# Three stages of a layered transformer kernel: residual sums written straight into the resident stream

## The chip, the cores and the metric

The kernel runs on one core of a Trainium2 chip. The metric is the time of one execution on the device, in microseconds (us); lower is better. All engines of the core run their own instruction streams and meet at semaphores: TensorE (PE) multiplies and transposes, VectorE (DVE), ScalarE (ACT) and GpSimd (POOL) compute on tiles, SyncE (SP) issues the transfers.

## What is computed

A batch of 32 sequences of 64 tokens with 128 features goes through four layers, each of a mixing step and a feed-forward step. Every step adds its result to the running x and takes the layer norm of x as its input. Cut to the steps around the change:

```python
def _layernorm(x, axis=-1, eps=1e-05):
    m = jnp.mean(x, axis=axis, keepdims=True)
    v = jnp.var(x, axis=axis, keepdims=True)
    return (x - m) / jnp.sqrt(v + eps)

x = x + _L0_xattn_ref(_layernorm(x), ctx_1024, ctx_1024, ...)   # gated recurrence: stage lstm
x = x + _L0_ffn_ref(_layernorm(x), ...)                          # mixture, 8 experts: stage moe0
x = x + _L1_xattn_ref(_layernorm(x), ctx_1024, _lenS2, ...)      # attention: stage att1
x = x + _L1_ffn_ref(_layernorm(x), ...)                          # mixture with shared expert: stage moe1
...                                                              # two further layers
```

Everything is fp32.

## The kernel before, in words

All 2048 tokens stay in SBUF for the whole run. `x_all` (128 x 16 x 128, fp32) is the resident stream x, `xT_all` the transposed layer norm of x. The tokens go in eight pairs of tiles (`PAIRS`), 256 tokens each; `pair(x_all, p)` is the 128 x 256 slice of pair p. The stages run one after the other, each over all pairs, in software loops (`Fori`) in which the loop's register gives the pair, with a first and a last pass outside the loop. The order of the work of each engine is written out by hand, and every dependence is a semaphore; inside DVE a `drain` stands between an instruction and one that reads its result.

Each stage ends a pair in the same way. DVE forms the new x of the pair, takes its statistics (`norm_stats`: two `bn_stats` L301, two `bn_aggr` L304, then the variance plus epsilon into `var`, L306, which releases POOL). POOL computes the inverse root (`take_root`, L332). DVE then applies it (`norm_apply`, two instructions at L313) into `xn`; TensorE transposes `xn` (L343) and ACT stores it in `xT_all` (L354). In the code this is a first part (sum and statistics) and an `ending`, with other work of DVE between them, and in the loops both belong to the pair before the current one.

Where the new x is formed:

- stage lstm: `scaled` adds the recurrence's result and x into the buffer `xr` (L626), takes the statistics of `xr`, and then copies `xr` into `x_all` (L629). After it come `scans` (from L565) or `ending`.
- stage moe0: `add_up` sums the experts into `xr` (two reductions, L810), adds x (L812), adds the bias product from the PSUM bank `ybank` (L815), copies `xr` into `x_all` (L817), then takes the statistics. `weigh` (from L772) follows, then `ending`, then `combine` (L802), which empties the banks that TensorE fills at L712.
- stage att1: `end_residual()` without a bias gives the two parts: the sum of `ybank` and x into `xr` (L1643), the copy `keep_stream` (L1637), the statistics. `divide` (L1388) scales queries and keys for TensorE's transposes (L1241) between the two parts.
- stage moe1, which the change doesn't touch: `sum_up` adds `ybank` into `x_all` in place (L1034), and statistics and `norm_apply` read `x_all` itself.

`end_residual("l3_bout")` of a later stage, ffn2 and tern keep `xr`, since they write x plus a bias into the stream (L1635) while the norm reads x without it.

Of the kernel before, what the change touches and what calls it, by code (L numbers as in the profile page):

```python
# [19 lines left out]
ALU = mybir.AluOpType  # L20
# [13 lines left out]
BUMP = 64  # L34
# [58 lines left out]
def build_program(nc, wpack, x_in, ctx_in, ctxT_in, rows_in, moeb_in, lens_in, mask_in, tern_in, scale_in, out,  # L93
                  layers=8):
    es = ExitStack()
    with es:
        def sb(name, shape, dt=F32):
            return es.enter_context(nc.sbuf_tensor(name, shape, dt))

        def sem(name):  # L100
            return es.enter_context(nc.semaphore(name))
# [12 lines left out]
        x_all = sb("x_all", [P, TILES, D])  # L114
# [3 lines left out]
        neg_len = sb("neg_len", [P, T])  # L118
# [7 lines left out]
        xn = sb("xn", [P, 2, D])  # L126
        xr = sb("xr", [P, 2, D])
# [27 lines left out]
        def bank(i):  # L155
            return big[:, i, :]

        ybank = bank(6)[:, 0:PT].rearrange("p (u d) -> p u d", u=2)
# [5 lines left out]
        def row(name, n=2):  # L164
            i = ROWS.index(name)
            return rows[:, i:i + 1, :].to_broadcast([P, n, D])

        def pair(ap3, p):

            return ap3[:, bass.ds(2 * p, 2), :]  # L170
# [15 lines left out]
        y_filled = sem("y_filled")  # L186
        xn_ready = sem("xn_ready")
        xt_filled = sem("xt_filled")
# [18 lines left out]
        def pipelined(these, mixing, inputs, late, tail=[]):  # L207


            s = stage([])  # L210
            s.pro = stage(inputs + late, 1)
            s.body = stage(these + inputs + mixing + late + tail, PAIRS - 1)
            s.epi = stage(these + mixing + tail, 1)
            return s
# [10 lines left out]
        def moe_units(nu, nd, lag):  # L225
# [4 lines left out]
            for d in downs:  # L230
# [4 lines left out]
                if d == nd - 1:  # L235
# [8 lines left out]
        att1 = pipelined(scores4, mixing8, [(f"tok{u}{c}", "a") for u in range(2) for c in range(4)],  # L244
                         values4 + [(f"turn{u}{c}", "av"[c % 2]) for u in range(2) for c in range(4)])
# [51 lines left out]
        def norm_stats(v, src, held=main):  # L297

            st, mv, var, _ = held
            for u in range(2):  # L300
                v.bn_stats(st[:, u, :], src[:, u, :])  # L301
            v.drain()
            for u in range(2):
                v.bn_aggr(mv[:, u, :], st[:, u, :])  # L304
            v.drain()
            v.tensor_scalar(var, mv[:, :, 1], 1e-5, None, ALU.add).then_inc(var_ready, 1)  # L306

        def norm_apply(v, src, dst, value, held=main):

            _, mv, _, rstd = held  # L310
            v.wait_ge(rstd_ready, value)
            for u in range(2):
                ins = v.tensor_scalar(dst[:, u, :], src[:, u, :], mv[:, u, 0:1], rstd[:, u:u + 1],  # L313
                                      ALU.subtract, ALU.mult)
            return ins
# [10 lines left out]
        def root(s, p, k):  # L326
            return p * roots[s][1] + (roots[s][0] + k)
# [28 lines left out]
        def g_of(s, p):  # L356

            return p + PAIRS * stages_run.index(s)
# [57 lines left out]
        lstm_n2 = work[:, 4864:5120].rearrange("p (g e) -> p g e", g=8)  # L416
# [137 lines left out]
        def lstm_vector(v):  # L554
            s = lstm
# [64 lines left out]
            def scaled(p):  # L620
                v.wait_ge(*h_lstm["hroot"].at(p, 1))
                v.tensor_tensor(lstm_n, lstm_n, lstm_hq[:, :, None].to_broadcast([P, 8, 32]), ALU.mult)
                v.drain()
                v.tensor_tensor(lstm_n2, lstm_n, lstm_ow.rearrange("p u (h e) -> p (u h) e", h=4), ALU.mult)
                v.drain()
                v.tensor_tensor(xr[:], lstm_n2.rearrange("p (u h) e -> p u (h e)", u=2), pair(x_all, p), ALU.add)  # L626
                v.drain()
                norm_stats(v, xr)
                v.tensor_copy(pair(x_all, p), xr[:])  # L629

            def ending(p):
                v.wait_ge(xt_filled, g_of(s, p) + BUMP)
                norm_apply(v, xr, xn, root(s, p, 1)).then_inc(xn_ready, 1)

            def part(ring, i, p, this, nxt, last=True):
                v.drain()
                if this:
                    exponent(ring, i)
                if nxt:
                    magnitude(ring, i, p + 1)  # L640
                if this:
                    decayed(ring, i, p)
                if this and last:
                    scaled(p - 1)
                if nxt:
                    scans(p + 1)
                if this:
                    if last:
                        ending(p - 1)
                    divided(ring, i, p)  # L650
            steps_lstm(v, part)
            scaled(PAIRS - 1)
            ending(PAIRS - 1)


# [13 lines left out]
        def moe(tag, s, pre, experts, chunks, func, layer):  # L669
# [70 lines left out]
            def vector(v):  # L740
# [66 lines left out]
                def add_up(p):  # L807

                    for u in range(2):
                        v.reduce_sum(xr[:, u, :], pr[:, u, :, :].rearrange("p e d -> p d e"), AX)  # L810
                    v.drain()
                    v.tensor_tensor(xr[:], xr[:], pair(x_all, p), ALU.add)  # L812
                    v.drain()
                    v.wait_ge(y_filled, p + yb(s))
                    v.tensor_tensor(xr[:], ybank, xr[:], ALU.add)  # L815
                    v.drain()
                    v.tensor_copy(pair(x_all, p), xr[:])  # L817
                    norm_stats(v, xr)

                def ending(p):  # L820
                    v.wait_ge(xt_filled, g_of(s, p) + BUMP)
                    ins = norm_apply(v, xr, xn, root(s, p, 1))
                    if layer == 1:
                        v.drain()
                        ins = v.tensor_tensor(pair(tok_all, p), xn[:], row("sa_bo"), ALU.add)
                    ins.then_inc(xn_ready, 1)

                def step(p, last=True):
                    v.drain()
                    sort(p)  # L830
                    if last:
                        add_up(p - 1)
                    weigh(p)
                    if last:
                        ending(p - 1)
                    combine(p)
# [4 lines left out]
                with v.Fori(1, PAIRS) as p:  # L841
                    step(p)
                add_up(PAIRS - 1)
                ending(PAIRS - 1)

            def pool(g, p):
# [235 lines left out]
        def yb(s):  # L1082

            return ystages.index(s) * PAIRS + 1
# [546 lines left out]


        def keep_stream(v, p, bias):
            if bias:
                v.tensor_tensor(pair(x_all, p), xr[:], row(bias), ALU.add)  # L1635
            else:
                v.tensor_copy(pair(x_all, p), xr[:])  # L1637

        def end_residual(bias=None):

            def first_part(v, s, p):
                v.wait_ge(y_filled, p + yb(s))
                v.tensor_tensor(xr[:], ybank, pair(x_all, p), ALU.add)  # L1643
                v.drain()
                keep_stream(v, p, bias)
                norm_stats(v, xr)

            def second_part(v, s, p):
                v.wait_ge(xt_filled, g_of(s, p) + BUMP)
                norm_apply(v, xr, xn, root(s, p, 1)).then_inc(xn_ready, 1)  # L1650
            return first_part, second_part
# [82 lines left out]
        def ffn_vector(v):  # L1734
# [7 lines left out]
            def step(p, last=True):  # L1742
                v.drain()
                v.wait_ge(y_filled, p + yb(s))
                v.tensor_tensor(xd, ybank, pair(tok_all, p), ALU.add).then_inc(y_read.sem, 1)
                v.drain()
                norm_stats(v, xd, inner)
                if last:
                    outer(p - 1)
                norm_apply(v, xd, xd, root(s, p, 1), inner)  # L1750
                v.drain()
                v.tensor_tensor(xd, xd, row("ln3_g"), ALU.mult)
                v.drain()
                v.tensor_tensor(xd, xd, row("ln3_b"), ALU.add)
                v.drain()
                v.tensor_tensor(xr[:], xd, pair(x_all, p), ALU.add)
                v.drain()
                norm_stats(v, xr)
                keep_stream(v, p, "tern_b")
# [95 lines left out]
        h3["values"] = Handoff("l3_values", 1)  # L1855
        h3["spread"] = Handoff("l3_spread", 2)
        end3 = end_residual("l3_bout")


# [367 lines left out]
        prog = {}  # L2227
# [8 lines left out]
        if moe0 in run:  # L2236
            prog[moe0] = moe("m0", moe0, "m0", 8, 2, ACT.Gelu, 0)
        if att1 in run:
            prog[att1] = attention("a1", att1, "a1_wq", "a1_wk", "a1_wv", "a1_wo", True, 2, neg_len, end_residual())
        if moe1 in run:  # L2240
            prog[moe1] = moe_shared(moe1)
        if satt in run:
# [326 lines left out]
```

## Time and profile before

| | us |
|---|---|
| median of 3 runs | 1338.88 |
| lowest, highest | 1337.35, 1341.19 |
| the profiled execution | 1337.23 |
| its span, first to last instruction | 1335.5 |

| engine | busy us | share of the span | instructions |
|---|---|---|---|
| PE | 1049.8 | 79% | 11888 |
| DVE | 927.0 | 69% | 2053 |
| ACT | 600.0 | 45% | 1169 |
| POOL | 215.0 | 16% | 226 |

The profile is of one execution. By the order of time, stage lstm runs from about 43 to 164 us, moe0 to about 305, att1 to about 555, moe1 to about 668. Busy shares are averages over stages with different limits; what a change in a stage is worth is read from the chain of work that ended last and from the order of time in that stage.

### The profile page before, as it was taken

The numbers are of one execution on the slowest core, as the hardware profiler recorded it, in microseconds if no ns is written. First come the engines' busy times: TensorE is split into PE (matmuls) and PEld (weight loads), VectorE is DVE, ScalarE is ACT, GpSimd is POOL, SyncE is SP. The second block draws the span as 40 slices with busy tenths as digits, with TensorE's granted clock in tenths as the row PEclk, the third lists the DMA queues.
The fourth block names the chain that finished last, engine by engine and source line by source line (L and its number), as shares of the span: only waits on it lengthen the run. The fifth ranks groups of instructions, "written<-read, shape, count | busy, mean of one in ns | idle before, by whom it ended". The sixth has DMA issues, their size and how long they took to land.

```text
span 1335.5 us, 32718 instructions
## 1 busy us (share of the span) xinstructions
PE 1049.8 (79%) x11888; PEld 823.5 (62%) x11888; DVE 927.0 (69%) x2053; ACT 600.0 (45%) x1169; POOL 215.0 (16%) x226
## 2 busy tenths in 40 slices
PE   1666499997888888589989999879999672588756
PEld 1433388884655656478867787658787551366646
DVE  3788757778899989445557676686867378666645
ACT  1333244446666666233346665346665230144333
POOL 2222322220012110223100000000000121243100
PEclk9756599998999999689999999899999796599868
DMA  9200000000000000000000000000000000000001
GB/s 365 105 0 0 1 0 0 0 0 1 2 0 0 0 0 1 1 1 0 1 2 1 0 0 1 2 2 0 0 0 1 1 0 0 0 1 0 0 1 31
DMA packets 4891, 17.48 MB, mean 13 GB/s; under 512 B 601, under 2 KB 2786, under 8 KB 4194
## 3 DMA queue, kind: packets, MB, share of 16 engines
q1 hardware_dynamic: 4834, 16.70, 3.3%
q8 instruction: 38, 0.62, 0.2%
q14 instruction: 19, 0.16, 0.0%
HBM read 15.65 MB, written 1.05 MB: 13 GB/s over the span
## 4 chain that ended last, share of the span: by engine, by line
PE 33%; issue 23%; DVE 23%; DVEq 13%; ACT 2%; POOL 2%; POOLq 1%; PEldq 1%; PEld 0%; ACTq 0%
PE banks L1480 5%; PE banks L1518 3%; PE banks L1490 3%; DVEq L1135 3%; PE banks L934 3%; PE banks L712 3%; PE banks L1467 2%; PE banks L1147 2%; DVE small L1378 2%; DVE small L1109 1%; DVEq L1108 1%; PE banks L1506 1%; DVE xn L313 1%; DVE weights L1388 1%; PE banks L343 1%
## 5 line engine op out<-in xcount | busy, mean ns | idle before, releaser
L332 POOL TENSOR_TENSOR rstd<-var,nhalf 128x2 f32<-128x2 f32 x72 | 57.4, 798 | 521.0 <-DVE var L306 514.1
L343 PE MATMUL banks<-ident,xn 128*128 128x128 f32 x160 | 38.6, 330 | 86.8 <-DVE xn L313 50.3
L1568 ACT ACTIVATE work<-banks 128x512 f32<-128x512 f32 x128 | 74.7, 600 | 70.4 <-PE banks L1480 70.4
L354 ACT ACTIVATE xT_all<-banks 128x256 f32 (+1 forms) x80 | 31.3, 391 | 153.9 <-PE banks L343 152.9
L1128 ACT ACTIVATE work<-work 128x1024 f32<-128x1024 f32 x64 | 67.7, 1057 | 59.8 <-DVEq L1124 32.8
L1480 PE MATMUL banks<-xT_all,weights 128*128 (+1 forms) x384 | 86.3, 381 | 1.4 <-ACT work L1561 0.9
L1603 DVE TENSOR_TENSOR work<-banks,neg_mask 128x512 f32<-128x512 f32 x64 | 40.7, 685 | 64.1 <-PE banks L1467 63.6
L343 PEld LDWEIGHTS banks<-ident,xn 128*128 128x128 f32 x160 | 20.4, 160 | 102.1 <-DVE xn L313 46.5
L1147 PE MATMUL banks<-ident,work 128*128 128x128 f32 x512 | 69.6, 286 | 16.3 <-DVE work L1138 11.1
L735 ACT ACTIVATE work<-banks,weights 128x256 f32<-128x256 f32 x128 | 53.8, 471 | 62.3 <-PE banks L702 61.4
L1480 PEld LDWEIGHTS banks<-xT_all,weights 128*128 128x128 f32 x384 | 71.9, 191 | 13.3 <-issue 1.8
L1147 PEld LDWEIGHTS banks<-ident,work 128*128 128x128 f32 x512 | 61.1, 147 | 23.0 <-DVE work L1138 13.8
L1518 PEld LDWEIGHTS banks<-weights,work 128*128 128x128 f32 x512 | 59.3, 194 | 15.2 <-ACT work L1561 14.9
L712 PE MATMUL banks<-weights,work 128*128 128x128 f32 x512 | 63.1, 276 | 6.4 <-DVE work L802 5.9
L712 PEld LDWEIGHTS banks<-weights,work 128*128 128x128 f32 x512 | 60.9, 191 | 10.6 <-ACT work L735 9.6
L1518 PE MATMUL banks<-weights,work 128*128 128x128 f32 x512 | 61.9, 279 | 3.8 <-ACT work L1561 3.8
L702 PE MATMUL banks<-xs,weights 128*128 128x256 f32 x256 | 61.8, 391 | 0.0
L1138 DVE TENSOR_TENSOR work<-work,small 128x1024 f32<-128x1024 f32 x48 | 58.8, 1225 | 3.6
L1555 ACT ACTIVATE work<-banks 128x512 f32<-128x512 f32 x64 | 34.7, 594 | 57.5 <-PE banks L1506 57.5
L313 DVE TENSOR_SCALAR xn<-xr,mv,rstd 128x128 f32<-128x128 f32 x128 | 41.5, 391 | 26.1 <-POOL rstd L332 23.7
L1154 ACT ACTIVATE work<-banks 128x512 f32<-128x512 f32 x96 | 52.2, 627 | 14.1 <-PE banks L1147 13.9
L1134 DVE TENSOR_REDUCE small<-work 128x16 f32<-128x1024 f32 x48 | 58.2, 1212 | 0.0
(313 smaller groups left out, 2521.2 us busy)
## 6 DMA issues: line engine op xcount, KB each, us to landing
weights<-wpack SPq DMA_DIRECT2D x1, 5381.5 KB, 29.2
weights<-wpack SPq DMA_DIRECT2D x1, 2060.0 KB, 10.2
weights<-wpack SPq DMA_DIRECT2D x1, 2049.0 KB, 14.6
weights<-wpack SPq DMA_DIRECT2D x1, 1160.5 KB, 16.9
ctxT_all<-ctxT_in SPq DMA_DIRECT2D x1, 1024.0 KB, 7.0
out<-x_all SPq DMA_DIRECT2D x8, 128.0 KB, 1.8
rows<-rows_in SPq DMA_DIRECT2D x1, 832.0 KB
weights<-wpack SPq DMA_DIRECT2D x1, 385.0 KB, 6.5
```

Of the source, the lines that this page charges most:

```text
L313: ins = v.tensor_scalar(dst[:, u, :], src[:, u, :], mv[:, u, 0:1], rstd[:, u:u + 1], ALU.subtract, ALU.mult)
L332: g.tensor_tensor(rstd, var, nhalf[:, 0:2], ALU.pow).then_inc(rstd_ready, 1)
L343: ins = pe.transpose(xtbank[:, u * P:(u + 1) * P], xn[:, u, :], ident[:])
L702: ins = pe.matmul(bk[:, (c % 2) * PT:(c % 2 + 1) * PT], upw[:, c, :], xs[:], start=True, stop=True)
L712: ins = pe.matmul(bk[:, (2 * u + e % 2) * D:(2 * u + e % 2 + 1) * D], hT[:, e * chunks + c, u * P:(u + 1) * P], dnw[:, e * chunks + c, :], ...
L1128: act.activation(sm[:, u, :], sm[:, u, :], ACT.Exp, scale=scale).then_inc(h["exp"].sem, 1)
L1134: v.reduce_sum(rs[:, u, :], every, AX)
L1138: v.tensor_tensor(every, every, rs[:, u, :, None].to_broadcast([P, 16, S]), ALU.mult) \
L1147: ins = pe.transpose(bank(s.bank(name))[:, c * P:(c + 1) * P], sm[:, u, 512 * half + c * P:512 * half + (c + 1) * P], ident[:])
L1480: ins = pe.matmul(bank(ring.bank(f"qk{c}"))[:, j * PT:(j + 1) * PT], wt[:, 2 * (c % 4) + j, :], cols(src, p), start=True, stop=True)
L1518: ins = pe.matmul(ybank[:, u, :], oT[:, u, c, :], wo[:, c, :], start=(c == 0), stop=(c == 7))
L1568: act.activation(dst.rearrange("p c t -> p (c t)"), bank(ring.bank(f"qk{c}")), ACT.Copy) \
```

## The change

In three stages the residual sum is written into `x_all` instead of `xr`, the statistics and `norm_apply` read `x_all`, and the copy from `xr` is gone. The new `end_in_place` takes the place of `end_residual()` without a bias; `keep_stream` keeps its form with a bias. In moe0 `xr` still takes the experts' sum.

```diff
@@ lstm_vector
-                v.tensor_tensor(xr[:], lstm_n2.rearrange("p (u h) e -> p u (h e)", u=2), pair(x_all, p), ALU.add)
-                v.drain()
-                norm_stats(v, xr)
-                v.tensor_copy(pair(x_all, p), xr[:])
+                v.tensor_tensor(pair(x_all, p), lstm_n2.rearrange("p (u h) e -> p u (h e)", u=2), pair(x_all, p),
+                                ALU.add)
+                v.drain()
+                norm_stats(v, pair(x_all, p))
...
-                norm_apply(v, xr, xn, root(s, p, 1)).then_inc(xn_ready, 1)
+                norm_apply(v, pair(x_all, p), xn, root(s, p, 1)).then_inc(xn_ready, 1)
@@ moe, add_up and ending
-                    v.tensor_tensor(xr[:], xr[:], pair(x_all, p), ALU.add)
+                    v.tensor_tensor(pair(x_all, p), xr[:], pair(x_all, p), ALU.add)
                     v.drain()
                     v.wait_ge(y_filled, p + yb(s))
-                    v.tensor_tensor(xr[:], ybank, xr[:], ALU.add)
-                    v.drain()
-                    v.tensor_copy(pair(x_all, p), xr[:])
-                    norm_stats(v, xr)
+                    v.tensor_tensor(pair(x_all, p), ybank, pair(x_all, p), ALU.add)
+                    v.drain()
+                    norm_stats(v, pair(x_all, p))
...
-                    ins = norm_apply(v, xr, xn, root(s, p, 1))
+                    ins = norm_apply(v, pair(x_all, p), xn, root(s, p, 1))
@@ keep_stream and the ends
-            if bias:
-                v.tensor_tensor(pair(x_all, p), xr[:], row(bias), ALU.add)
-            else:
-                v.tensor_copy(pair(x_all, p), xr[:])
-
-        def end_residual(bias=None):
+            v.tensor_tensor(pair(x_all, p), xr[:], row(bias), ALU.add)
+
+        def end_in_place():
+
+            def first_part(v, s, p):
+                v.wait_ge(y_filled, p + yb(s))
+                v.tensor_tensor(pair(x_all, p), ybank, pair(x_all, p), ALU.add)
+                v.drain()
+                norm_stats(v, pair(x_all, p))
+
+            def second_part(v, s, p):
+                v.wait_ge(xt_filled, g_of(s, p) + BUMP)
+                norm_apply(v, pair(x_all, p), xn, root(s, p, 1)).then_inc(xn_ready, 1)
+            return first_part, second_part
+
+        def end_residual(bias):
@@ the stage att1
-            prog[att1] = attention("a1", att1, "a1_wq", "a1_wk", "a1_wv", "a1_wo", True, 2, neg_len, end_residual())
+            prog[att1] = attention("a1", att1, "a1_wq", "a1_wk", "a1_wv", "a1_wo", True, 2, neg_len, end_in_place())
```

## Rows read from the trace of the kernel before

**Rows 1.** Groups by line, 43 to 560 us: busy us, mean ns, idle before.

```profile
L817 DVE COPY x_all<-xr 128x256 f32 (+1 forms) x8 | 2.4, 294 | 0.6
L1637 DVE COPY x_all<-xr 128x256 f32 (+1 forms) x8 | 2.3, 294 | 0.6
L629 DVE COPY x_all<-xr 128x256 f32 (+1 forms) x8 | 2.3, 285 | 0.0
```

**Rows 2.** Chain that ended last: start us, us, what.

```profile
64.81 0.27 DVE x_all L629
...
139.88 0.26 DVE x_all L629
...
186.75 0.29 DVE x_all L817
...
303.02 0.29 DVE x_all L817
...
518.55 0.29 DVE x_all L1637
...
552.44 0.29 DVE x_all L1637
```

**Rows 3.** Order of time, DVE, one lstm pass: start us, us, instruction, [idle before].

```profile
93.52 0.42 DVE L626 TENSOR_TENSOR xr<-work,x_all 128x256 f32<-128x256 f32 x1 [0.20 <-issue]
94.02 0.48 DVE L301 BATCH_NORM_STATS2 st<-xr 128x6 f32<-128x128 f32 x2
...
94.90 0.17 DVE L306 TENSOR_SCALAR var<-mv 128x2 f32<-128x2 f32 x1
94.98 0.28 DVE L629 COPY x_all<-xr 128x256 f32 x1
95.18 0.44 DVE L565 SCALAR_TENSOR_TENSOR work<-work 128x256 f32<-128x256 f32 x1
```

**Rows 4.** Order of time, DVE, one moe0 pass.

```profile
219.52 0.42 DVE L812 TENSOR_TENSOR xr<-xr,x_all 128x256 f32<-128x256 f32 x1 [0.29 <-issue]
...
220.52 0.29 DVE L817 COPY x_all<-xr 128x256 f32 x1
220.73 0.48 DVE L301 BATCH_NORM_STATS2 st<-xr 128x6 f32<-128x128 f32 x2
...
221.61 0.17 DVE L306 TENSOR_SCALAR var<-mv 128x2 f32<-128x2 f32 x1
221.72 0.16 DVE L772 TENSOR_TENSOR small<-small 128x2 f32<-128x2 f32 x1
```

**Rows 5.** Order of time, DVE, one att1 pass.

```profile
429.17 0.29 DVE L1637 COPY x_all<-xr 128x256 f32 x1
429.38 0.48 DVE L301 BATCH_NORM_STATS2 st<-xr 128x6 f32<-128x128 f32 x2
```

**Rows 6.** Order of time, DVE, last passes of lstm and of att1.

```profile
153.07 0.28 DVE L629 COPY x_all<-xr 128x256 f32<-128x256 f32 x1
154.04 0.60 DVE L313 TENSOR_SCALAR xn<-xr,mv,rstd 128x128 f32<-128x128 f32 x2 [0.69 <-POOL rstd L332]
...
544.87 0.60 DVE L313 TENSOR_SCALAR xn<-xr,mv,rstd 128x128 f32<-128x128 f32 x2 [0.88 <-POOL rstd L332]
```

**Rows 7.** Order of time, DVE, one moe1 pass, which works in place.

```profile
603.35 0.42 DVE L1034 TENSOR_TENSOR x_all<-banks,x_all 128x256 f32 x1
603.87 0.49 DVE L301 BATCH_NORM_STATS2 st<-x_all 128x6 f32 x2
...
604.75 0.17 DVE L306 TENSOR_SCALAR var<-mv 128x2 f32<-128x2 f32 x1
```

**Rows 8.** Order of time, PE, one pass each of lstm, moe0, att1.

```profile
99.70 0.44 PE L343 MATMUL banks<-ident,xn 128*128 128x128 f32 x2 [2.28 <-DVE xn L313]
...
225.38 2.05 PE L712 MATMUL banks<-weights,work 128*128 128x128 f32 x16 [0.85 <-DVE work L802]
...
432.86 1.96 PE L1241 MATMUL banks<-ident,weights 128*128 128x128 f32 x16 [1.10 <-DVE weights L1388]
```

## The prediction, made before the changed kernel ran

> **What bounds the kernel now.** I read the grouped instructions first, for how many copies there are and what one costs; then the chain of work that ended last, for which of them lie on the path; then the order of time on VectorE (DVE) around one copy of each stage, for what really separates its neighbours; last the TensorE lines after them, for a second path close behind.
>
> The three stages hold 24 copies of xr into x_all, eight to a stage, of 285 ns (L629) or 294 ns (L817, L1637) [rows 1]. The chain passes through 21 of them: L629 in the six passes that lie in the loop (first and last shown), L817 in all eight, L1637 in the six of the loop and once more at the stage's end [rows 2]. So DVE sets the pace in all three stages, in turn with TensorE in moe0, and each of these copies delays the next pass. The other three are covered: the last two L629 (one shown) run while POOL makes the root, for which DVE then still waits 0.69 us, and the seventh pair of att1 is finished beside TensorE's mixing, where DVE waits 0.88 us for POOL [rows 6]. These three give back nothing: the root starts from var, which for L629 comes before the copy, and the chain doesn't go through the seventh att1 pair. If that cover were gone they would add 2 x 0.17 and 0.21, 0.55 us.
>
> **The change part by part.** The durations are those of the profiled execution: span 1335.5 us, 1337.2 us with what lies around it; the median of the runs is 1338.9, 1.7 above it. I subtract the same microseconds from all three.
>
> *What a removed copy frees* is not its duration but the distance between the starts of its neighbours, since the next instruction starts before the copy has ended. In lstm the copy stands behind the variance (L306): L306 starts at 94.90, L629 at 94.98, L565 at 95.18, 0.28 us from L306 to L565 [rows 3]. Without it L565 follows L306 directly; it waits for a semaphore by a computed value, as L772 does behind L306 in moe0, and there the distance is 0.11 us (221.61 to 221.72) [rows 4]. So 0.17 us go. In moe0 and att1 the copy stands between the finished sum and the statistics: 220.52 to 220.73 and 429.17 to 429.38, 0.21 us each [rows 4, 5]. The sum's drain stays, before the statistics instead of before the copy.
>
> *What is added.* No instruction that computes. But x_all is addressed by the loop's pair number, xr is not. The sums, the two statistics instructions and the two L313 now read or write by a register. moe1 already does exactly this, so its rows bound the cost: from L1034 to the first L301 it is 0.52 us there (603.35 to 603.87) [rows 7], against 0.50 in lstm (93.52 to 94.02) [rows 3]: 0.02 us for a register address behind a drain. From the first L301 to L306 it is 0.88 us in both (603.87 to 604.75; 94.02 to 94.90) [rows 3, 7]: the second tile's address costs nothing, worked out while the first runs. The other end is the 0.29 us before L812, which also follows a drain and has a register address [rows 4], against the 0.20 before L626 [rows 3]. I take moe1's 0.02, as its instructions are the very ones that the change makes. In lstm that is paid once a pass (the sum had its register address already), in moe0 twice (its second sum reads xr now and will read x_all), in att1 once. Writing the sum into x_all instead of xr costs nothing: L1034 takes 0.42 us as the old sums do [rows 3, 7]. Behind the loops the addresses are constants and nothing is added.
>
> *The sum.* lstm: 6 x (0.17 - 0.02) = 0.90. moe0: 7 x (0.21 - 0.04) + 0.21 = 1.40. att1: 6 x (0.21 - 0.02) + 0.21 = 1.35. Together 3.65 us. Not a single wait, semaphore or DMA is added or moved, and what waits for DVE on POOL and TensorE waits for less. In moe0 and att1 the variance comes 0.2 us earlier too, so the root is earlier by the same, and where DVE waits for it (the stage ends) the gain is kept.
>
> *What is late next.* TensorE waits for DVE in all three: 2.28 us for xn in lstm, 0.85 us for the emptied bank in moe0, 1.10 us for the scaled queries and keys in att1 [rows 8]. A shift of 0.15 to 0.2 us leaves all of them waiting, so nothing takes the place of DVE within a pass.
>
> The Trainium skill speaks here on what a copy is worth: VectorE: DVE Perf Modes, Terms, says that the pipeline is flushed after every DVE operation and the next can't issue until it is empty. By that rule a removed copy would free its whole duration and the sum would be some 2 us larger; the trace does not agree, for L301 starts 0.21 us after L817, which lasts 0.29 [rows 4].
>
> **The rivals.**
>
> *The gain is given back later, or was covered.* A stage may hand its lead to a wait that I don't see move: TensorE's bank order, POOL's staging between stages, or the clock of later stages. For it: at stage boundaries the chain leaves DVE for TensorE and POOL. Against it: 19 of the 21 copies lie in loops with the idle times above, and the passes of one stage follow at equal distance (64.81 to 139.88 is five passes of 15.01) [rows 2]. Half of the gain lost gives 1337.1, all of it 1338.9.
>
> *The whole copy goes.* If the overlap of copy and successor is only one of recorded times, and the successor really does its work after the copy's end, a removed copy frees 0.285 or 0.294: 6 x (0.285 - 0.02) + 7 x (0.294 - 0.04) + 6 x (0.294 - 0.02) + 2 x 0.294 = 1.59 + 1.78 + 1.64 + 0.59 = 5.6 us, so 1333.3. Against it stand the starts in rows 3 to 5. This is also what the rule of VectorE: DVE Perf Modes in the Trainium skill would give.
>
> *Register addresses stall DVE, and it gets slower.* The mechanism: each operand by a register makes DVE's sequencer compute before it can issue, and in a loop that costs what it costs before L626, where 0.20 us pass against the 0.08 from L306 to L629 without such an operand, so 0.12 us [rows 3]. The place: the two L301 and two L313 of all 19 loop passes, 4 x 0.12 = 0.48 us a pass, 9.1 us in all, against a gross gain of 6 x 0.17 + 15 x 0.21 = 4.2. That is 1338.9 + 4.9 = 1343.8. It decides as soon as an instruction costs over 4.2 / 76 = 0.055 us. For it: the gap before L812 is even larger. Against it: moe1 does the same four in each pass and shows 0.02 us for all of the statistics [rows 7].
>
> *The change does nothing.* Could the copies stay in another form, as the sum of moe0 that still starts in xr? No: the diff takes out all 24 and adds none, so this has no chance of its own.
>
> **How the numbers follow.** My forecast, 3.65 us saved, gives 1335.2 us (the profiled execution's span would be 1331.9). It has a chance of 0.68. The runs of before lie between 1337.35 and 1341.19, so a median of three can miss by 1 to 2 us either way, and this case reaches from 1333.3 to 1337.3. Given back or covered: 0.18. The whole copy: 0.09. Slower by register addresses: 0.05.
> A measurement of this kernel tells about 0.3% from no change, 4.0 us, so the line for faster is at 1334.9 and that for slower at 1342.9. The forecast stands at 0.27%, just short of the line: of its 0.68 I give 0.32 to the faster side, and of the 0.09 for the whole copy 0.08: faster 0.40. Slower is the register case, 0.05. Same has the rest, 0.55. For eight in ten the range goes down to 1332.6 (into the whole copy) and up to 1338.8 (over most of what may be given back), leaving out the register case and the ends.
>
> **What would show it.** L629, L817 and L1637 gone, DVE with 2029 instructions instead of 2053. Passes shorter by 0.15 us in lstm, 0.17 in moe0, 0.19 in att1, read from the starts of one line in successive passes. From the sum's start to the first L301: 0.52 us in all three loops, and 0.88 from there to L306. The start of moe1 3.65 us earlier than now, and the same distance from there to the end. If the passes shorten by this and the end does not move, it was given back behind moe1; if the gaps before L301 or L313 grow to 0.2 us, the register case holds; if a pass shortens by the copy's full duration, the second rival. The forecast is wrong in its size if the 0.02 us of moe1 do not carry over to loops whose sum follows a drain, and in its sign only if they are over 0.055 for every instruction.

## The result

The changed kernel takes 1331.38 us, the median of 6 runs (1329.51 to 1332.75), against 1339.84 for the kernel before (6 runs, 1337.16 to 1341.19) taken with it: ratio 0.9944, 95% interval 0.993 to 0.9958. That is faster by 0.56%, 7.5 us of 1338.9 (the two medians here lie 8.5 apart), where 3.65 us were forecast, and it lies below the predicted range. The profiled execution's span is 1329.2 us.

The engines' row of the page of the kernel after (busy us, share of the span, instructions):

```profile
PE 1048.3 (79%) x11888; PEld 822.3 (62%) x11888; DVE 922.9 (69%) x2029; ACT 599.5 (45%) x1169; POOL 215.2 (16%) x226
```

The 24 copies are gone from DVE (2053 to 2029), and its busy time falls by 4.1 us. That is nearer to 24 distances between neighbours (8 x 0.17 and 16 x 0.21, 4.7 us) than to the copies' 7.0 us of [rows 1], since time in which two instructions overlap is busy once.

Order of time on DVE in the kernel after, one pass each of lstm, moe0 and att1 (start us, us, instruction, idle before it and what ended it):

```profile
93.21 0.42 DVE L626 TENSOR_TENSOR x_all<-work,x_all 128x256 f32 x1 [0.20 <-issue]
93.71 0.49 DVE L301 BATCH_NORM_STATS2 st<-x_all 128x6 f32 x2
...
94.60 0.17 DVE L306 TENSOR_SCALAR var<-mv 128x2 f32<-128x2 f32 x1
94.70 0.43 DVE L565 SCALAR_TENSOR_TENSOR work<-work 128x256 f32<-128x256 f32 x1
...
218.81 0.42 DVE L812 TENSOR_TENSOR x_all<-xr,x_all 128x256 f32 x1 [0.19 <-issue]
219.41 0.42 DVE L815 TENSOR_TENSOR x_all<-banks,x_all 128x256 f32 x1 [0.17 <-issue]
219.91 0.49 DVE L301 BATCH_NORM_STATS2 st<-x_all 128x6 f32 x2
...
220.79 0.17 DVE L306 TENSOR_SCALAR var<-mv 128x2 f32<-128x2 f32 x1
...
410.04 1.23 DVE L1110 TENSOR_TENSOR work<-work,small 128x1024 f32<-128x1024 f32 x1
...
425.42 0.42 DVE L1639 TENSOR_TENSOR x_all<-banks,x_all 128x256 f32 x1
425.92 0.49 DVE L301 BATCH_NORM_STATS2 st<-x_all 128x6 f32 x2
...
426.80 0.17 DVE L306 TENSOR_SCALAR var<-mv 128x2 f32<-128x2 f32 x1
```

From the sum to the first L301 it is 0.50 us in all three stages, and 0.88 or 0.89 from there to L306: the register address costs not even the 0.02 us that was taken from [rows 7]. From L306 to L565 it is 0.10 where it was 0.28 [rows 3]. So much answers to the plan. Two lines don't. In moe0 the gap before L812, 0.29 us in [rows 4], is 0.19 now, and a new one of 0.17 stands before L815, which had none. And L1110 has no idle time before it, while the same instruction in the kernel before, a softmax step 16 us away from the edit, has one in each pass of att1. DVE before (the last two lines are the same instruction in successive passes):

```profile
411.90 1.22 DVE L1109 TENSOR_REDUCE small<-work 128x16 f32<-128x1024 f32 x1
413.30 1.23 DVE L1111 TENSOR_TENSOR work<-work,small 128x1024 f32<-128x1024 f32 x1 [0.18 <-issue]
...
443.09 1.23 DVE L1111 TENSOR_TENSOR work<-work,small 128x1024 f32<-128x1024 f32 x1 [0.18 <-issue]
```

The passes of the loops, from one L306 to the next, are 14.79 us for 14.97 in lstm, 16.68 for 16.87 in moe0 and 29.49 for 29.79 in att1. Starts of L306 in two successive passes of att1, before and then after:

```profile
370.68 0.17 DVE L306 TENSOR_SCALAR var<-mv 128x2 f32<-128x2 f32 x1
400.47 0.17 DVE L306 TENSOR_SCALAR var<-mv 128x2 f32<-128x2 f32 x1
```

```profile
367.83 0.17 DVE L306 TENSOR_SCALAR var<-mv 128x2 f32<-128x2 f32 x1
397.32 0.17 DVE L306 TENSOR_SCALAR var<-mv 128x2 f32<-128x2 f32 x1
```

Followed along these starts, after leads by 1.0 us at lstm's end, 1.8 at moe0's, 4.4 at the end of att1's loop, 5.3 at its last pair, 5.4 to 6.5 through moe1 and the two attention stages behind it, 7.0 in ffn2 and 6.3 at the end of the span. The sum has 0.9 and 2.3 us at the first two points, and 3.65 from att1's end on: there the lead is half as large again, and nearly twice the sum in ffn2.

### The profile page after: what moved, and what is told of

It reads as the page before. It is cut to its first block, busy times and chain, and to the rows that moved or that the text cites. A ratio compares the mean times of both kernels' runs of the same rounds, so it can differ in the third digit from the quotient of the medians.

```text
span 1329.2 us, 32713 instructions
## 1 busy us (share of the span) xinstructions
PE 1048.3 (79%) x11888; PEld 822.3 (62%) x11888; DVE 922.9 (69%) x2029; ACT 599.5 (45%) x1169; POOL 215.2 (16%) x226
## 4 chain that ended last, share of the span: by engine, by line
PE 32%; issue 24%; DVE 23%; DVEq 13%; POOL 2%; ACT 2%; PEld 1%; PEldq 1%; POOLq 1%; ACTq 0%
PE banks L1479 5%; PE banks L1517 3%; DVEq L1134 3%; PE banks L712 3%; PE banks L933 3%; PE banks L1489 2%; PE banks L1146 2%; PE banks L1466 2%; DVE small L1377 2%; PE banks L1505 2%; DVE small L1108 1%; DVEq L1107 1%; DVE weights L1387 1%; DVE xn L313 1%; DVEq L811 1%
## 5 line engine op out<-in xcount | busy, mean ns | idle before, releaser
L1137 DVE TENSOR_TENSOR work<-work,small 128x1024 f32<-128x1024 f32 x48 | 58.8, 1225 | 3.6
L1315 ACT ACTIVATE weights<-banks 128x512 f32<-128x512 f32 x64 | 41.0, 640 | 32.2 <-PE banks L1212 32.2
```

Of the source, the lines that this page charges most:

```text
L1137: v.tensor_tensor(every, every, rs[:, u, :, None].to_broadcast([P, 16, S]), ALU.mult) \
```

## The experiments

**The theory.** Some of DVE's idle times called "issue" belong to a place in its instruction stream, not to the instruction behind them. I counted DVE's instructions in the compiled kernels, drains and register instructions included. In the kernel before, the odd gaps stand at places 217 (L608), 347 (L812) and 477 (L1111): 130 apart each time, which I took for twice 65; what the true spacing is comes under The period. Each is long the first time its code is passed (0.44, 0.58, 0.44 us) and about 0.1 us longer than its neighbours in every later pass, where it falls on the instruction right behind a drain; elsewhere a running instruction hides it. Inside the loops the change takes out as many instructions as it adds for register addresses; at the stages' ends, where addresses are constants, it loses 2 in lstm, 1 in moe0 and 2 in att1. So place 347 now falls on L815, and place 477 into the middle of L1103, where it is hidden. **The rival:** the copies were worth more than their distance, or the edited instructions behave otherwise, and L1111 is a mere companion.

**Places restored.** The kernel after, with five drains that do nothing put back where five instructions were lost, outside the loops.

```diff
             steps_lstm(v, part)
+            v.drain()
+            v.drain()
             scaled(PAIRS - 1)
...
                 add_up(PAIRS - 1)
+                v.drain()
                 ending(PAIRS - 1)
...
                 v.drain()
+                v.drain()
+                v.drain()
                 end[0](v, s, PAIRS - 1)
```

> The changed kernel with five empty drains on DVE: two before the last pair of lstm, one before the last ending of moe0, two before the last pair of att1. Nothing is computed otherwise. Every DVE instruction behind a removed instruction then stands at the place in the instruction stream that it has in the kernel before (1636 instructions instead of 1631). Theory place (a removed copy is worth 0.17 us a pass in lstm and 0.2 in moe0 and att1, and the rest of the gain is a stall of DVE's issue that returns every 65 instructions and no longer falls behind a drain in att1): att1 passes go back from 29.49 to 29.59 us, the idle time of 0.18 us before the first softmax subtraction (L1111 of before) comes back and 0.44 in the first pass, and the ratio to the kernel before is 0.997 (4.2 us saved). Rival copy (the copies alone are worth all of it): passes stay at 29.49 and the ratio at 0.9944. Rival clock (the extra is the TensorE clock of the stages' ends): passes at 29.49 too, and the offsets at the ends of att1 and in ffn2 are what varies.

Measured: 1334.22 us (1328.92 to 1339.4, 12 runs), ratio 0.997 (0.9954 to 0.9987). The softmax step, numbered L1113 here, on DVE:

```profile
410.49 1.23 DVE L1113 TENSOR_TENSOR work<-work,small 128x1024 f32<-128x1024 f32 x1 [0.18 <-issue]
```

The gap is back, to the hundredth, and att1's pass is 29.59 us instead of 29.49; lstm stays at 0.18 and moe0 at 0.20 less than before. At 29.79 − 29.59 an att1 copy is worth 0.20. Five instructions that do nothing, none in a loop, take back 2.8 us by the medians (1334.22 against 1331.38). The two intervals just overlap, and the profiled spans don't separate the two kernels (1331.0 against 1329.2 and, repeated, 1330.9), so it is the passes that carry this reading. What is left, 0.3% or 4.0 us (1.7 to 6.2), is near the 3.65 that were forecast for the copies.

**The places alone.** The kernel before, all copies kept, with ten drains at the start of DVE's stream, where it waits for constants anyway.

```diff
+            for _ in range(10):
+                v.drain()
             v.wait_ge(consts_made, 1)
```

> The kernel before, its arithmetic untouched, with ten empty drains at the start of DVE's stream, where DVE waits 9.9 us for POOL's constants. All later DVE instructions stand ten places further. Theory place: the issue stalls that fall behind a drain in the loops of lstm (0.20 us before L608), moe0 (0.29 before L812) and att1 (0.18 before L1111) vanish or shrink: some 0.12, 0.1 and 0.1 us a pass, with the first-pass stalls of 0.4 to 0.6 us some 4 us in all, ratio 0.997. Rivals copy and clock: no difference, ratio 1.000.

Measured: 1333.91 us (8 runs), ratio 0.9972 (0.9952 to 0.9992). L608 on DVE, after ten drains, has no idle time before it; the kernel before had 0.20:

```profile
85.65 0.42 DVE L608 TENSOR_REDUCE small<-work 128x8 f32<-128x256 f32 x1
```

Passes are shorter by 0.12 us in lstm, 0.04 in moe0 and 0.10 in att1, and the first long stall at L608 is gone. In moe0 that is less than the 0.1 expected: L812 gains 0.1, but L753, on which the place now falls, comes 0.04 us later in the pass. Moving the code by ten places, with every copy still there, gains as much as taking the copies out with the code held in place.

**Ahead of att1 alone.** The kernel before, with `for _ in range(4): v.drain()` ahead of att1's code on DVE.

> The kernel before with four empty drains ahead of att1's DVE code. Theory place: the stall of 0.18 us before L1111 in att1's loop goes (it falls four instructions earlier, where a sum is still running): passes 29.69 instead of 29.79 us, first pass 0.37 shorter, some 1 us saved there, lstm and moe0 unchanged; the whole kernel 0 to 1 us faster, since the same shift may put other stalls behind drains later. Rivals copy and clock: passes stay at 29.79.

Measured: 1337.66 us (12 runs), ratio 0.9998 (0.9982 to 1.0014). The passes of att1 are 29.69 us, 0.10 less, and 1.0 us is gained by the end of its loop; then 0.5 us goes again over att1's last pair and moe1's start, 0.3 at the attention stage behind it, and by the end of the next one nothing is left. So a microsecond gained in att1 can be given back later.

**One stage at a time.** The kernel before with the diff's lines for a single stage; first lstm.

> The kernel before with the change in stage lstm alone; later DVE instructions stand two places earlier. Theory place: lstm passes 14.79 instead of 14.96 us; in moe0 the stall moves from the first residual sum (0.29 us before L812) to the second (L815), passes as before (16.87); in att1, whose code is untouched, the 0.18 us before L1111 goes and the passes are 29.69 instead of 29.79. 1 us from the copies, 1 us from att1's place: ratio about 0.9985. Rival copy: att1 passes stay at 29.79.

Measured: 1335.68 us (10 runs), ratio 0.9985 (0.9967 to 1.0003). DVE in att1, which this kernel doesn't edit:

```profile
410.54 1.23 DVE L1111 TENSOR_TENSOR work<-work,small 128x1024 f32<-128x1024 f32 x1
...
440.23 1.23 DVE L1111 TENSOR_TENSOR work<-work,small 128x1024 f32<-128x1024 f32 x1
```

The edit in lstm, two instructions fewer at its end, takes the gap away from L1111 250 us later, and att1's pass is 29.69 us. In moe0 the gap moves from L812 to L815, as in after, and the pass stays at 16.88. The interval holds 1, so here too the trace decides and not the time.

> The kernel before with the change in stage att1 alone; up to att1's end every DVE instruction keeps its place. Theory place: att1 passes 29.59 us (0.20 for the copy), not 29.49, since the 0.18 us before L1111 stays; lstm and moe0 as before; ratio about 0.9985 (1.4 us from the copies, the rest from where stalls fall behind att1). Rival copy: passes 29.49 as in the changed kernel, 0.30 for the copy.

Measured, att1 alone: 1334.57 us (10 runs), ratio 0.9979 (0.9962 to 0.9996). Nothing ahead of att1's loop is moved, and the gap is kept while the copy is gone:

```profile
412.58 1.23 DVE L1111 TENSOR_TENSOR work<-work,small 128x1024 f32<-128x1024 f32 x1 [0.18 <-issue]
```

Its passes are 29.59 us: 0.20 for the copy and nothing for the place.

> The kernel before with the change made in moe0 alone; lstm and att1 keep their copies. Behind the loop of moe0 the DVE stream loses one instruction, so the code of att1 and all later code stands one place earlier than in before. Copy theory: the passes of moe0 16.87 to 16.68 us (as in e1), those of lstm 14.97 as before; 8 copies at 0.20 us, 1.6 us saved by the end of moe0 less what TensorE's first block takes or gives. Theory that places matter: att1's place 477 falls one instruction later than L1111, onto L1113 or its like behind a running instruction, so the stall of 0.18 us before L1111 goes and att1's passes, which this kernel does not edit, are 29.69 us instead of 29.79 and the first stall of 0.44 is gone: 1.0 us more. So: ratio 0.998 with both, 0.9988 with the copies alone. Rival (stalls belong to the edited instructions): att1's passes stay at 29.79.

Measured, moe0 alone: 1336.88 us (12 runs), ratio 0.9989 (0.9975 to 1.0004). moe0's passes are 0.20 us shorter, and att1's, one place earlier, are 29.69 us without the gap. The interval holds 0.998, 0.9988 and 1, so the verdict rests on the trace, not on the time. L306 in two passes of att1:

```profile
368.74 0.17 DVE L306 TENSOR_SCALAR var<-mv 128x2 f32<-128x2 f32 x1
398.43 0.17 DVE L306 TENSOR_SCALAR var<-mv 128x2 f32<-128x2 f32 x1
```

**The period.** The kernel before with 64 drains at the start: a period of 64 would leave the gaps on their instructions, one of 65 moves each by one instruction.

> The kernel before with 64 empty drains at the start of DVE's stream, to tell the period of the stalls. By the places counted in three kernels (217, 347, 477) it is 65: L608 and L1111 then stand one place ahead of where the stall falls, which is a drain with a longer instruction ahead of it, or one that is not behind a drain, and the 0.20 us before L608 and 0.18 before L1111 go. If the period is 64, both stay as they are (0.20 and 0.18) and the time is that of the kernel before.

Measured: 1333.74 us (10 runs), ratio 0.9971 (0.9954 to 0.9987). L608 has no idle time (86.07 us, behind L606), L812 has 0.20 for 0.29, and L1111 has none; passes are shorter by 0.12 to 0.13 us in lstm, 0.22 in moe0 and 0.10 in att1. (In moe0 half of this is L812; the rest is a shorter wait for TensorE at L744, 0.57 for 0.69 us, which nothing here explains.) A period of 64 is out. But 65 is not shown by it, and the same trace speaks against 65: there is a new long stall in the first pair of lstm, ahead of the loop.

```profile
56.40 0.42 DVE L608 TENSOR_REDUCE small<-work 128x8 f32<-128x256 f32 x1 [0.43 <-issue]
```

The places 217, 347 and 477 count the labels that the compiled file has at the start and behind the end of each loop. They are targets of branches and leave no record in the trace. Two of them lie between each two of the three places; without them the places are 191, 319 and 447, and the distance is 128. Counted so, the L608 of this line stands at 191 with the 64 drains ahead of it, where the loop's L608 stood in before, while that one has moved to 255, half a period on, and has no gap. By 65 the new stall belongs one instruction later. Behind att1 the two counts part in the kernel before, too:

```profile
1067.61 0.48 DVE L301 BATCH_NORM_STATS2 st<-xr 128x6 f32<-128x128 f32 x2 [0.45 <-issue]
```

This L301 is at 1252 with the labels, 1035 behind 217 and so no multiple of 65 away from it; without them it is at 1215, eight times 128 behind 191. In ten of the traces (before, after, their repeats and the kernels with drains) the distance from one instruction that computes to the next, where the second waits for no semaphore, can be set beside the shortest one at the same spot in kernels of like code. It is longer by 0.28 us or more 51 times in a first pass, and all 51 have such a place (191, 319 and so on, up to 1599) between the two instructions, as against 16 for multiples of 65 behind 217. So the period is 128 instructions, labels left out. Where the text above has 217, 347 and 477, these are 191, 319 and 447; what it says of lost instructions and of four, five, ten or eleven drains holds by either count, since both move alike.

**After, moved on.** The kernel after with 11 drains at the start, to take the last gaps off L608 and L815.

> The changed kernel with eleven empty drains at the start of DVE's stream. Theory place: lstm and moe0 lose the stalls that they still have in the changed kernel (0.2 us before L608, 0.17 before L815), 0.12 and 0.1 us a pass and 0.3 to 0.4 us once each, some 3.5 us in all: ratio to the kernel before 0.992. Rivals copy and clock: 0.9944, as the changed kernel.

Measured: 1330.08 us (1327.55 to 1330.82, 6 runs), ratio 0.9935 (0.9919 to 0.9951). Passes are shorter than before by 0.30, 0.28 and 0.31 us. By moe1 it leads by 7.1 us, of which 1.3 go again in the second attention stage behind it; after loses 0.5 there and the kernel with places restored 1.0, though att1 alone gains 1.2. Its median is the lowest of all the kernels here, and 0.992 lies in its interval; but it is only 1.3 us under that of after, where 3.5 were expected, and the intervals overlap.

> The changed kernel with 62 empty drains at the start of DVE's stream, the number for which, by the period of 65, the fewest stalls fall behind a drain (none in a loop, two outside). Theory place: one or two us less than with eleven drains (1330.1): ratio to the kernel before 0.992. Rival copy: 0.9944 as the changed kernel, or more by what the drains themselves cost, if POOL's constants don't cover them.

Measured, with 62 drains: 1331.65 us (1326.93 to 1334.0, 12 runs), ratio 0.9952 (0.9937 to 0.9968); 0.992 was a miss. The loops did what was expected (0.31, 0.34 to 0.39 and 0.31 us less a pass, but for the first of moe0, no gap at L608, L815 or L1110). Outside them they did not. By the period of 65 two stalls were to fall behind a drain; the trace has six long ones, of 0.40 to 0.45 us, before L610, L306, L1017, L1135, L2126 and L1137, and the one before L1017 lies in moe1's loop and comes again with 0.19. All six are at places of the period of 128. Two of them:

```profile
58.27 0.17 DVE L610 TENSOR_SCALAR small<-small 128x8 f32<-128x8 f32 x1 [0.43 <-issue]
...
1028.66 1.23 DVE L1137 TENSOR_TENSOR work<-work,small 128x1024 f32<-128x1024 f32 x1 [0.45 <-issue]
```

Besides, POOL's first iota starts 1.36 us later, and all of DVE's stream waits for it. POOL in the kernel with 11 drains, then in the one with 62:

```profile
9.58 0.14 POOL L2336 IOTA ix<- 128x16 int32 x1 [8.34 <-issue]
```

```profile
10.94 0.14 POOL L2336 IOTA ix<- 128x16 int32 x1 [9.70 <-issue]
```

The drains don't do it as such: with 64 of them in the kernel before, the iota starts at 9.57. The cause of this late start is open, and so is whether all 12 runs had it.

**The same kernels once more**, for what belongs to the kernel and what to the execution.

> The kernel after once more, unchanged, for a second profile. If TensorE's clock at the ends of stages belongs to the execution and not to the kernel, blocks that differed between before and after will differ between the two profiles of after: the first block of moe0 (L702, 6.40 us in after, 5.64 in before), the last pair of att1 (L1255, 2.81 against 3.68 us) and the first block of ffn2 (L1712 of the second pass, 1.94 to 1.99 against 3.66 us). If it belongs to the kernel, all three repeat within 0.1 us. The stalls of DVE do not depend on the clock: L608 0.20, L815 0.17 and no stall before L1110 in every pass, cold ones 0.44 and 0.46, again. Passes 14.79, 16.68 and 29.49 us.

> The kernel before once more, unchanged, for a second profile. If TensorE's clock at the stage ends belongs to the execution: L702's first block (5.64 us), L1256 of the last pair of att1 (3.68 us) and the first blocks of ffn2 (3.75, 3.78, 3.66 us) come out otherwise. If it belongs to the kernel, they repeat within 0.1 us. Stalls of DVE: L608 0.20, L812 0.29, L1111 0.18 in each pass, 0.44, 0.58 and 0.44 the first time, again. Passes 14.97, 16.87 and 29.79 us.

Measured: 1332.59 and 1336.53 us, spans 1330.9 and 1334.8. The gaps and the passes repeat to 0.01 us, in att1 to 0.02. TensorE's first block in moe0 and, in after, its block of the last pair of att1 do not; in before the first takes 5.41 us for 5.64 and the second repeats within 0.1 (3.60 for 3.68). PE of after:

```profile
160.58 6.40 PE L702 MATMUL banks<-xs,weights 128*128 128x256 f32 x16
...
539.91 2.81 PE L1255 MATMUL banks<-work 64*64 64x64 f32 x128
```

PE of after, repeated:

```profile
160.17 5.58 PE L702 MATMUL banks<-xs,weights 128*128 128x256 f32 x16
...
539.46 3.62 PE L1255 MATMUL banks<-work 64*64 64x64 f32 x128
```

0.8 us less at one end and 0.8 more at the other, in the same kernel. The granted clock explains both; for the first, stretches of 4 us from 160 us on (engines' busy us, then PEclk), after and then its repeat:

```profile
160.00:164.00 4.00, 4.00 (x12) 3.37 (x12) 2.63 (x12) 0.84 (x2) 0.70 (x1) 0.50 0.01 4
164.00:168.00 4.00, 4.00 (x20) 3.45 (x20) 1.14 (x11) 2.52 (x6) 2.90 (x1) 0.74 0.00 0
```

```profile
160.00:164.00 4.00, 4.00 (x11) 3.28 (x12) 2.64 (x16) 0.87 (x3) 0.77 (x2) 0.50 0.02 4
164.00:168.00 4.00, 4.00 (x27) 3.74 (x27) 1.22 (x9) 2.48 (x6) 2.83 (x1) 1.00 0.00 0
```

Between the stages TensorE has little to do (0.30 and 0.70 us of the 4 from 156 to 160) and is granted 0.50 of full speed, 1.2 GHz. It is back at 2.4 GHz at 166.1 us in one execution and at 164.0 in the other, about two microseconds sooner. For the block in att1 it is the other way round: the stretch 540 to 542 us has 0.62 in after and still 0.50 in its repeat. The lead of 1.8 us at moe0's end in the first profile of after, less than the sum of its passes, is this; in the repeat it is 3.1 over the same profile of before, and 2.8 over before's own repeat.

ffn2 is another matter. Its third block at L1703 takes 3.66 us in before, with a granted clock of 0.57 in that stretch, and 1.99 in after with 1.00. In the repeats the clock is 0.64 and 1.00 and the block takes 3.59 and 1.99 us, so in these two kernels it came out alike twice. PEclk in before and in after for 4 us around that block:

```profile
1070.00:1074.00 4.00, 3.66 (x8) 2.53 (x8) 3.28 (x13) 1.08 (x3) 0.69 (x1) 0.57 0.00 0
```

```profile
1064.00:1068.00 4.00, 2.98 (x15) 2.23 (x16) 3.27 (x13) 2.06 (x5) 0.92 (x2) 1.00 0.00 0
```

The lead grows here by 1.4 us in after and by 1.4 to 1.5 in its repeat; also by 1.4 in the kernel with places restored and with 11 drains, by 1.7 with att1 alone and 1.6 with moe0 alone; by 0.5 with ten or 64 drains in the kernel before and by 0.1 to 0.2 with four ahead of att1. With lstm alone it shrinks by 2.0: there three such blocks, not one, take 3.42 to 3.54 us, in a profiled execution (1338.2) that is 2.5 us above that kernel's median. Whether this goes with the kernel, in a stage that no diff touches, is therefore open: only before and after were profiled twice. What decides it was not settled.

## Why the prediction was wrong

**The copies.** "What a removed copy frees", the distance between neighbours' starts, was right: 0.18 us in lstm for 0.17, 0.20 in moe0 and att1 for 0.21. Both the whole-copy rival and the flush rule of the Trainium skill's VectorE: DVE Perf Modes (Terms), by which 0.285 to 0.294 would have gone, are out: with places held the passes lose 0.18, 0.20 and 0.20. The sum of 3.65 us meets 4.0 (1.7 to 6.2) there.

**The address.** The 0.02 us of [rows 7] was a term too many: 0.50 us, not 0.52, from sum to statistics. Without it the sum would be 0.52 us larger (26 times 0.02), 4.2 us, which doesn't repair the forecast. The register rival is dead: not one of the new addresses shows a gap of its own. The gap before L812 that spoke for it was a stall of the place, as its fall from 0.29 to 0.19 with the address kept shows.

**The step that failed** is "What is added. No instruction that computes", and the sum built on it, in which every instruction that is not edited keeps its gaps. Instructions at the stages' ends were lost, the code behind them moved, and what that does to the stalls was put at nothing without a reason. The term for att1, 6 x (0.21 − 0.02) + 0.21 = 1.35, measured 6 x 0.30 = 1.8 in the loop, 0.11 of each pass from L1111's gap, and 0.37 more at its first pass, where L1111's long stall of 0.44 went. Behind att1 0.27 before L1002, 0.25 before L313, 0.45 before L1120 and 0.37 before L306 are gone too, and 0.45 before L301 is 0.38 before L306 now; 0.46 before L1011 came, with 0.20 in its second pass, and 0.46 before L1033, which the view puts down to TensorE but which stands at such a place (831). The rows that should have warned me were at hand: an idle time called "issue" that is 0.29 before L812 and 0.20 before L626, two instructions of the same kind, is not a property of the kind. The passes of lstm say it too: the average of 15.01 us in the prediction hides that the first is 15.21 and the others 14.95 to 14.97, and the 0.24 more is L608's first stall. I took the gap before L812 as the upper bound for a register address and didn't ask what else it could be.

**What is late next** held inside the passes. PE of the kernel after, the waits that answer to [rows 8] in lstm, moe0 and att1:

```profile
99.21 0.44 PE L343 MATMUL banks<-ident,xn 128*128 128x128 f32 x2 [2.10 <-DVE xn L313]
...
224.57 2.05 PE L712 MATMUL banks<-weights,work 128*128 128x128 f32 x16 [0.66 <-DVE work L802]
...
399.92 1.96 PE L1240 MATMUL banks<-ident,weights 128*128 128x128 f32 x16 [0.90 <-ACT work L1355]
```

2.28, 0.85 and 1.10 us have become 2.10, 0.66 and 0.90: TensorE comes earlier by what DVE does, and still waits. In att1 the wait is put down to ACT now, so little is left there for DVE to give.

**Given back later** was a true rival in part: most kernels that lead into the second attention stage lose 0.3 to 1.4 us there, and the four drains ahead of att1 ended at nothing. It did not decide, because in after ffn2 gave 1.4 us the other way. At the stage ends TensorE's clock moved single blocks by 0.8 us, either way from execution to execution. None of this was in the sum, and only the first was in the range.

**What adds up and what doesn't.** By the ratios the copies alone are worth 4.0 us and the places 3.5 more (0.997 less 0.9944); by the medians it is 4.7 and 2.8. Either way the two make up the 7.5, but how they share it is not known to better than 1 or 2 us. Of the places' part the traces show 0.9 us in att1's loop and its first pass. Behind att1 the idle times called "issue" at such places are 1.95 us with places restored and 1.04 in after, or 1.50 with the one before L1033, so 0.45 to 0.9 more at most, since not all of them need lie on the path. The rest, 1.0 to 2.2 us, I give no cause for. The profiled executions of before, 1337.23 and 1336.53, lie under its medians of 1338.8 to 1339.8, so the spans differ by 3.9 to 6.3 us only, and why the median of before lies further above its two profiles than that of after does is open.

## What to carry to other kernels

Where a profile shows a short idle time called "issue" that its like elsewhere doesn't have, count where it stands in the engine's stream before giving it to the instruction. An edit that adds or removes instructions shifts the code behind it, in loops it never touches; such a shift here was worth about as much as the edit itself. Count the instructions that run, without labels, and test a period at places far apart, not only where it was found. So compare an edit also with its places restored, and try a few idle instructions at a place that waits anyway: with 10, 11 and 64 of them DVE's first instruction behind the wait came within 0.1 us of that of before (12.29, 12.40 and 12.38 for 12.35).

## What the hardware showed

DVE can stall at every 128th instruction of its stream by place, branch labels not counted (places 191, 319, 447 and on to 1599 in these kernels): about 0.1 us each time the place is passed again in a loop, and about 0.37 us the first time, where the profile shows up to 0.58 us of idle time. Where an instruction is still running or DVE waits for another engine, nothing or only a part of it shows. The stalls fit code that is fetched in pieces, but that is argued, not shown: only the places and the durations are. A register address on an instruction of DVE behind a drain costs nothing that these traces resolve. When TensorE's granted clock goes back from 1.2 to 2.4 GHz after a stage's start differs by about two microseconds between executions of one kernel (166.1 and 164.0 us), and with it single blocks by 0.8 us.
